# In-projection begun on one half of the tokens, an accumulator kept half by half, and V weights loaded in four pieces

## What is computed

```
# layer 0: attention, 16 heads of 32
xn = layer_norm(x) * norm_w + norm_b
att = softmax(q @ k.T + mask);  y = att @ v            # q, k, v = xn @ weights + bias
h = layer_norm(y) * (1 + scale) + shift                # scale, shift from the condition
x1 = x + silu(h) @ out_w + out_b
# layer 1: a selective state-space layer (Mamba), inner width 1024, 16 states
xn = layer_norm(x1) * (1 + scale) + shift
x_in, z = split(xn @ in_proj_w.T)
u = silu(causal_conv4(x_in) + conv_b)
dt, B, C = split(u @ x_proj_w.T);  dt = softplus(dt @ dt_proj_w.T + bias)
h_t = h_{t-1} * exp(dt_t * A) + dt_t * u_t * B_t;  y_t = sum_n(h_t * C_t)
out = x1 + gate * ((y + u * D) * silu(z)) @ out_proj_w.T
```

## Time and profile before

| | us |
|---|---|
| median of 3 runs | 6713.71 (6713.31 to 6713.74) |
| the profiled execution, its own time | 6710.81 |
| its span | 6709.0 |
| PE busy | 6107.8 (91%) |
| DVE busy | 5862.3 (87%) |
| ACT busy | 4556.3 (68%) |
| POOL busy | 3156.5 (47%) |
| mean granted TensorE clock | 0.947 |
| mean DMA rate | 162 GB/s |

### The profile page before, as it was taken

The page is one execution under the profiler, slowest core; times in us unless marked ns, Lnnn a source line. Parts: engine busy times, 40 slices in busy tenths (PEclk is TensorE's granted clock), DMA queues, the critical chain, the costliest instruction groups (busy, mean ns, idle before and its releaser), DMA issues.

```text
span 6709.0 us, 114578 instructions
## 1 busy us (share of the span) xinstructions
PE 6107.8 (91%) x43104; PEld 3983.7 (59%) x43104; DVE 5862.3 (87%) x7115; ACT 4556.3 (68%) x6528; POOL 3156.5 (47%) x1538
## 2 busy tenths in 40 slices
PE   5998999988999889989899899998899988999876
PEld 2774558645585556845568455774558645685554
DVE  0788999799997999979999799988999799996995
ACT  2775678657785677846778467865778667785663
POOL 0104881068701786019840389205881068601883
PEclk8999999999999999999999999999999999999967
DMA  3525885368934689238873498535894368924775
GB/s 143 181 82 160 203 207 153 107 163 195 236 104 141 160 205 235 77 141 177 211 200 95 135 208 209 162 98 159 196 214 142 119 162 199 244 69 144 171 149 127
DMA packets 428533, 1087.52 MB, mean 162 GB/s; under 512 B 49560, under 2 KB 49688, under 8 KB 423792
## 3 DMA queue, kind: packets, MB, share of 16 engines
q1 hardware_dynamic: 249440, 656.81, 30.2%
q0 software_dynamic: 160144, 390.09, 29.8%
q10 hardware_dynamic: 18432, 33.56, 1.4%
HBM read 570.16 MB, written 241.71 MB: 121 GB/s over the span
## 4 chain that ended last, share of the span: by engine, by line
PE 66%; DVE 16%; issue 7%; DMA 5%; POOL 4%; ACT 2%; SPq 1%; DVEq 0%; POOLq 0%; ACTq 0%
PE ps L1240 38%; PE ps L1349 12%; DVE area_h L1161 9%; PE ps L1488 8%; PE ps L1290 3%; POOL area_s L690 3%; DVE area_acc L1171 3%; DMA area_acc<-area_w 2%; DMA z_keep<-z_st 1%; DMA k_stack<-qk_keep 1%; PE ps L1292 1%; DVE area_dt L1149 1%; DVE norm_st L998 1%; DVE area_h L1129 1%; PE ps L1435 1%
## 5 line engine op out<-in xcount | busy, mean ns | idle before, releaser
L690 POOL TENSOR_TENSOR area_s<-area_u,area_s 128x1024 f32<-128x1024 f32 x1024 | 2548.6, 2578 | 536.1 <-DVE area_u L1152 372.4
L1161 DVE TENSOR_TENSOR_SCAN area_h<-ps,area_s 128x1024 f32<-128x1024 f32 x1024 | 2341.1, 2286 | 48.0 <-POOL area_s L690 39.7
L1488 PEld LDWEIGHTS ps<-ident,area_h 128*128 128x128 f32 x8192 | 987.0, 150 | 796.5 <-DVE area_acc L1171 425.5
L1488 PE MATMUL ps<-ident,area_h 128*128 128x128 f32 x8192 | 1190.5, 292 | 231.1 <-DVE area_acc L1171 152.6
L812 ACT ACTIVATE area_s<-area_s,negmax 128x1024 f32<-128x1024 f32 x1024 | 1180.7, 1153 | 253.4 <-DVE negmax L1058 245.9
L1058 DVE CUSTOM_DVE_ANT_0 area_s<-ps,area_dt 128x1024 f32<-128x1024 f32 x1024 | 1243.6, 1216 | 102.7 <-PE ps L1240 102.0
L879 ACT ACTIVATE ps<-area_dt,negA 128x1024 f32<-128x1024 f32 x1024 | 1147.0, 1120 | 240.2 <-DVE area_h L1161 102.3
L678 POOL TENSOR_TENSOR area_s<-area_s 128x1024 f32<-128x1024 f32 x64 | 180.2, 2815 | 2306.9 <-ACT area_s L854 2306.9
L863 ACT ACTIVATE area_w<-ps,C_nat 128x512 f32<-128x512 f32 x1024 | 704.9, 688 | 703.2 <-PE ps L1488 668.2
L1349 PE MATMUL ps<-ident,area_s 128*128 128x128 f32 x8192 | 1066.9, 273 | 0.4
L1349 PEld LDWEIGHTS ps<-ident,area_s 128*128 128x128 f32 x8192 | 959.9, 141 | 140.6 <-issue 7.0
(11 more groups left out here) (124 smaller groups left out, 5413.4 us busy)
## 6 DMA issues: line engine op xcount, KB each, us to landing
area_acc<-area_w POOLq DMA_DIRECT2D x256, 1024.0 KB, 8.8
area_s<-b_rows SPq DMA_DIRECT2D x256, 512.0 KB, 5.3
q_stack<-qk_keep SPq DMA_DIRECT2D x512, 128.0 KB, 2.8
k_stack<-qk_keep SPq DMA_DIRECT2D x512, 128.0 KB, 3.1
area_s<-z_keep SPq DMA_DIRECT2D x72, 512.0 KB, 4.4
qk_keep<-q_stack SPq DMA_DIRECT2D x128, 256.0 KB, 4.8
qk_keep<-k_stack SPq DMA_DIRECT2D x128, 256.0 KB, 4.8
y_keep<-area_acc POOLq DMA_DIRECT2D x8, 4096.0 KB, 13.9
```

What stands on the lines that cost most here:

```text
L690: pool.tensor_tensor(dbu[:, dl % 2, :], U[:, k // (NS * DL) * DL + dl, :], bb[:, q, :], ALU.mult).then_inc(s_dbu.sem, 1)
L1161: v.tensor_tensor_scan(out=hs[:, q, dl, :], data0=banks(2 * (dl % 2)), data1=dbu[:, dl % 2, :], initial=0.0, op0=ALU.mult, op1=ALU.add).th ...
L1488: last = nc.tensor.transpose(ps[:, 4 + n % 2, dl * P:(dl + 1) * P], hs[:, r % 2, dl, n * P:(n + 1) * P], ident[:, :])
```

## The change

Seven edits, in the code's terms:

1. **In-projection in halves.** `norm_pe` and `affine` take a half as argument. PE transposes n2's half 0 after out-projection product 6, before product 7. ACT does `affine` of half 0 after its two `root` of the next sequence's n0 and before `root(n2, b, 1)`. PE then does the token half 0 of channel groups 0 to 3, with the transposes of half 1 after group 2, and then waits for half 1. Half 1's transposes go to banks 1, 3, 5 and 7. Groups 4 to 7 run as before.
2. **n1's half 0 on ACT.** Its four normalising instructions move from DVE (L1019) to ACT, as activations; DVE keeps the shift and goes to half 1's statistics at once.
3. **Accumulator layout.** `area_acc` is now seen as (dg half, parity, 4 tiles, 512 columns). The four odd tiles of one dg are one run of 2048 words.
4. `du_keep` is stored and loaded in whole runs.
5. `y_keep` is read in two runs of 512 words for each tile instead of one of 1024.
6. **V weights** in four DMAs of 256 KB, after stores 7, 8, 9 and 10.
7. **Out-projection weights** are loaded in the attention stage, after the loads for head 13, instead of in the scan.

The diff, cut to its core:

```diff
-        acc = area_acc[:, :].rearrange("p (n d) -> p n d", n=NT)
-        piece = [acc[:, n, 512:1024] for n in range(NT)]
+        acc_parts = area_acc[:, :].rearrange("p (h e m c) -> p h e m c", h=DG, e=2, c=512)
+        acc = [acc_parts[:, :, n % 2, n // 2, :] for n in range(NT)]
+        piece = [acc[n][:, 1, :] for n in range(NT)]
...
-        n2 = Norm("norm2", n1.rows)
+        n2 = Norm("norm2", n1.rows, ((0, 1, 2, 3), (1, 3, 5, 7)))
...
-            def load_wv(inst):
-                sp.wait_ge(*s_fp.at(inst, N0_UNITS + QK_UNITS // 2))
-                sp.dma_start(wv, v_w.rearrange("(k p) c -> p k c", p=P)).then_inc(s_wv.sem, 16)
-            def load_wo(inst):
-                sp.wait_ge(*s_fp.at(inst, FIRST_V))
+            def load_wv(inst, k):
+                if k == 0:
+                    sp.wait_ge(*s_fp.at(inst, N0_UNITS + QK_UNITS // 2))
+                sp.dma_start(wv[:, k, :], v_w[k * P:(k + 1) * P, :]).then_inc(s_wv.sem, 16)
+            def load_wo():
                 sp.dma_start(wo, out_w.rearrange("(k p) c -> p k c", p=P)).then_inc(s_wo.sem, 16)
...
                         load_stack(g * HG + j + 2, j % 2)
+                load_wo()
...
-                    sp.dma_start(y_ring[:, n % 2, :], y_keep[:, n * DI:(n + 1) * DI]).then_inc(s_gyz[n % 2].sem, 16)
+                    sp.dma_start(y_ring[:, n % 2, :].rearrange("p (h c) -> p h c", h=DG), y_parts[:, :, n % 2, n // 2, :]).then_inc(s_gyz[n % 2].sem, 16)
...
-                        sp.dma_start(du_keep.rearrange("p (n d) -> p n d", n=NT), acc[:, :, 512:1024]
+                        sp.dma_start(du_keep, area_acc[:, NT * 512:]
                                      ).then_inc(s_dus.sem, 16)
...
-                        if u == QK_UNITS // 2 - 1:
-                            load_wv(b + 1)
+                        if QK_UNITS // 2 - 1 <= u < QK_UNITS // 2 - 1 + KD:
+                            load_wv(b + 1, u - QK_UNITS // 2 + 1)
                         if u == QK_UNITS - 1:
-                            load_wo(b + 1)
                             parts_stored(b + 1)
...
-                    pool.dma_start(acc_odd[:, :, dg * 512:(dg + 1) * 512], part[slot], accum_op=ALU.add
+                    pool.dma_start(acc_parts[:, dg, 1, :, :].rearrange("p m c -> p (m c)"), part[slot].rearrange("p m c -> p (m c)"), accum_op=ALU.add
                                    ).then_inc(s_ad.sem, 16)
...
+                root(n1, b, 0)
+                act.wait_ge(*n1.shift.at(b, 1))
+                _, _, _, rstd, nmr = n1.rows
+                for n in range(HALF):
+                    nc.scalar.activation(xhat[:, n, :], Y[:, n, :], ACT.Identity, bias=nmr[:, n:n + 1],
+                                         scale=rstd[:, n:n + 1]).then_inc(n1.xhat.sem, 1)
+                root(n1, b, 1)
...
                 root(n2, b, 0)
                 for hf in range(2) if b + 1 < B else ():
                     root(n0, b + 1, hf)
+                affine_n2(0)
                 root(n2, b, 1)
+                affine_n2(1)
...
-                normalise(n1, b, Y, 0)
+                shift_of(n1, b, 0)
...
                     last.then_inc(s_op.sem, 1)
-                norm_pe(n2, b)
+                    if n == NT - 2:
+                        norm_pe(n2, b, 0)
+                def in_product(n, th):
+                    for k in range(KD):
+                        done = mm(ps[:, 2 * (n % 4) + th, :], wx[:, k, n * P:(n + 1) * P],
+                                  xT[:, k, th * 512:(th + 1) * 512], k, KD - 1)
+                    return done
+                pe.wait_ge(*n2.ready.at(b, KD))
+                pe.wait_ge(*s_wx.at(b, 16))
+                for n in range(4):
+                    if n == 2:
+                        pe.wait_ge(*s_x1.at(b, NT - 1))
+                    in_product(n, 0)
+                    if n == 2:
+                        norm_pe(n2, b, 1)
                 pe.wait_ge(*n2.ready.at(b, 2 * KD))
-                pe.wait_ge(*s_wx.at(b, 16))
                 for n in range(ND):
                     if n >= 4:
                         pe.wait_ge(*s_c0.at(b, n - 3))
-                    for th in range(TB):
-                        for k in range(KD):
-                            last = mm(ps[:, 2 * (n % 4) + th, :], wx[:, k, n * P:(n + 1) * P],
-                                      xT[:, k, th * 512:(th + 1) * 512], k, KD - 1)
-                    last.then_inc(s_ip.sem, 1)
+                        in_product(n, 0)
+                    in_product(n, 1).then_inc(s_ip.sem, 1)
```

More of the change, by code:

```diff
@@ L561, in _ @@
                         sp.wait_ge(*s_gp.at(b, NU - 1))
-                        sp.dma_start(acc[:, 0:NT:2, 512:1024], du_keep.rearrange("p (n d) -> p n d", n=NT)[:, 0:NT:2, :]
+                        sp.dma_start(acc_parts[:, 1, 0, :, :], du_parts[:, 0, :, :]
                                      ).then_inc(s_dul[0].sem, 16)
@@ L567, in _ @@
                         sp.wait_ge(*s_gp.at(b, NU))
-                        sp.dma_start(acc[:, 1:5:2, 512:1024], du_keep.rearrange("p (n d) -> p n d", n=NT)[:, 1:5:2, :]
+                        sp.dma_start(acc_parts[:, 1, 1, 0:2, :], du_parts[:, 1, 0:2, :]
                                      ).then_inc(s_dul[1].sem, 16)
@@ L571, in _ @@
                         sp.wait_ge(*s_ga.at(b, 16 * NT // 2))
-                        sp.dma_start(acc[:, 5:NT:2, 512:1024], du_keep.rearrange("p (n d) -> p n d", n=NT)[:, 5:NT:2, :]
+                        sp.dma_start(acc_parts[:, 1, 1, 2:4, :], du_parts[:, 1, 2:4, :]
                                      ).then_inc(s_dul[1].sem, 16)
@@ L750, in root, with affine @@
                 nc.scalar.activation(rstd[:, rows], rv[:, rows], ACT.Sqrt).then_inc(N.rstd.sem, 1)
-            def affine(N, b, gains, shifts, func):
-                for hf in range(2):
-                    for k in range(KD):
-                        act.wait_ge(*N.tp.at(b, hf * KD + k + 1))
-                        nc.scalar.activation(xT[:, k, hf * 512:(hf + 1) * 512], ps[:, hf * KD + k, :], func,
-                                             scale=gains(k), bias=shifts(k)).then_inc(N.ready.sem, 1)
+            def affine(N, b, hf, gains, shifts, func):
+                for k in range(KD):
+                    act.wait_ge(*N.tp.at(b, hf * KD + k + 1))
+                    nc.scalar.activation(xT[:, k, hf * 512:(hf + 1) * 512], ps[:, N.banks[hf][k], :], func,
+                                         scale=gains(k), bias=shifts(k)).then_inc(N.ready.sem, 1)
             def normalise_next(inst, n):
@@ L1034, in _ @@
             for hf in range(2):
-                shift_next(0, hf)
+                shift_of(n0, 0, hf)
             for b in range(B):
@@ L1168, in add @@
                     dve.wait_ge(*s_acc.at(b, k + 1 - DL))
-                    part = acc[:, n, dg * 512:(dg + 1) * 512]
+                    part = acc[n][:, dg, :]
                     c_col = C_nat[:, n, r:r + 1] if isinstance(r, int) else C_nat[:, n, bass.ds(r, 1)]
@@ L1374, in _ @@
                 pe.wait_ge(*s_yn.at(b, G * HG * 2))
-                norm_pe(n1, b)
+                for hf in range(2):
+                    norm_pe(n1, b, hf)
                 pe.wait_ge(*s_wo.at(b, 16))
```

66 lines of the change are left out of this document (32 added, 34 removed).

## The result

The changed kernel takes **6661.6 us** (median of 4 runs, 6657.9 to 6663.5), the kernel before 6713.5 in the same session: ratio 0.9923, 95% interval [0.9906, 0.994]. The prediction said 6658.7. The number is close, but the terms that led to it are not, and most of what follows is about that.

A forecast was written before the change was run, and what follows sets the result against it. PE was taken to bound the middle of a sequence, DVE the scan. Gains of 25 + 11 + 14 + 4 + 1 = 55 us off 6710.8, plus 2.9 to the median, gave 6658.7; range 6634 to 6688.

The forecast's parts named there:

- PE's side of the halves: In-projection: PE idles 0.6 us in place of 3.9, half 1's transposes follow three half groups of 3.45 us each.
- T+24.1: Start of convolution 0, counted in us from T, the end of the out-projection; 5.7 us later than before.
- DVE's pace: Convolution: DVE becomes the bound at 5.94 us for a group with its gap; the halves gain 25 us.
- the case with the bound of 33: Upper bound of the halves' gain: without the shared port PE bounds the stage again, about 1 us more for each sequence.
- The port rule: Convolution: DVE and POOL share one port pair under exclusive lock, so a group costs both engines' work, about 6.0 us.
- It fits, barely: Ring of y and z: z lands 12.3 us after convolution 0 starts, ACT wants it after 12.9; nothing to 10 us lost.
- the ring of y and z held the convolution at a pace of 6.5: In-projection rival: the halves gain nothing and only n1's 11 us are left, 6702 us; chance 0.06.
- V pieces and layout, 14 us: Scan: three quarters of the stalls about round 9 go, 14 us; bounds 0 to 18.4.
- du_keep, 4 us: Scan, round 2: longer runs shorten the last piece that gates POOL, half a us for each sequence; bounds 0 to 12.8.
- All stalls go: Scan rival: 8 KB runs speed accumulation; round 9 stalls vanish, half of round 2's, 5 us at the tail; 6639, chance 0.11.
- n1, 11 us: Norm 1: PE starts half 1's transposes sooner and without idle time, 1.4 us in each of eight sequences; bounds 6 and 15.
- The tail: End of the kernel, where the last accumulation of 9.70 us is alone on the path: 1 us gained, bounds -1 and 6.

The follow-up runs named there:

- the kernel with the ring split: The changed kernel with z's load issued before the wait for the store and z on semaphores of its own, y still in two runs: 6622.9 us, ratio 0.987.

## Why the prediction came out right, and where it was wrong

**PE's side of the halves**: right in each step. I said convolution 0 would start at T+24.1; it starts 22.0 us after the last residual add, which is itself some 1.8 us later. I said a gap of 0.6; it is 0.61.

**DVE's pace** of 5.94 us: "it stays when PE is no longer late" held, at 5.82 us wherever POOL's gating falls beside the group. The 0.12 us too much, in 64 groups, are 7.7 us, and the kernel with the ring split gains 32.0 in these two stages where I had 25. The halves alone gain 35.4: there some groups have no gating beside them, DVE is no longer the bound and PE is, as the case with the bound of 33 supposed. The port rule's "about 6.0 us" is a wrong sum: three times 1.28 and 2.39 are 6.2, and the group takes less.

**"It fits, barely" ... "Nothing, down to 10 us lost if y lands a us later"**: this is the step that failed, and it was worth more than any term of the sum. y landed only 0.7 us later than before, and the stage lost some 47 us (569.5 with the halves alone, 616.6 in the change), not 10. I had compared one load with one deadline; it is a closed ring. By the durations of before the trip is 0.4 for issues, 4.4 for z, 1.1 for SiLU, 2.6 for gating and 2.6 for the store, 11.1 us. Before, two groups of PE took 13.8; with the halves two groups of DVE take 11.6. So the slack fell from 2.7 us to 0.5, and the halves alone already used it up (trips of 12.5 on average), which they survive only because PE allows the last groups to be late. The change then adds 0.2 for y's issue, 0.9 to z behind y, and 1.9 to the store behind late loads: 14.1 us, near the mean of 14.5 in the trace. Of the 47 us, 35 are PE waiting for U ahead of the x-projection's parts. The other 12 fall, but for half a us, in the six sequences whose mean granted clock in this stage is under 1 (0.972 to 0.988; 1.00 in all with the halves alone). The prediction had named the signs itself, convolution groups of over 6.2 us, gaps of 0.5 us or more and ACT waiting for z, and all three are there. The rival "the ring of y and z held the convolution at a pace of 6.5" named the mechanism with a chance of 0.06 and the sum of 6702 that it gives with n1 alone; I had set the ring's price as a bound of 10 us in one place and as the loss of 25 in another, and had not asked what it costs when it is late in earnest.

**V pieces and layout, 14 us**, as three quarters of the stalls: all seven are gone (18.4), and each part alone would have taken 15 us of them or more. Costing them as one term hid that one of them was nearly superfluous there. **du_keep, 4 us**: the round-2 stall gave 1.1, which is within its scatter (12.8 us before, 12.9 with the layout alone, 14.5 with the V pieces alone). **Nothing for dg 0 and the attention**: that was the other failed step. The layout alone gives 10 us in each; "runs of 8 KB make the accumulation clearly faster" stood only in the rival "All stalls go", where I let it act on stalls and the tail alone.

**n1, 11 us**: 17.4, since the clock gain was undersized. I gave it "a little sooner", but PE's 32 transposes without a gap took 5.35 us against 3.14 + 3.68 before. Between traces this stage scatters from 119.2 to 126.3 us without the edit and from 103.6 to 106.4 with it. **The tail**, 1 us: 2.4 with the start. (The "6636" among the bounds leaves out the 2.9 us to the median; it should be 6639, which changes nothing in the range.)

So, gained against predicted, +6 (n1), -37 (halves and ring), +30 (scan and attention) and -1 (the rest) cancelled to -2 us. That the forecast came so close was luck, and is no evidence for its steps.

**A better version.** Any of the three cures (y in one run, z on its own semaphores, z's load before the wait) gives 6617 to 6623 us, about 40 us under the change and some 95 under the kernel before; they can't be told apart. z's load before the wait is the smallest edit.

## What to carry to other kernels

Where tiles go around a ring (load, compute, store, load again), compare the whole trip with as many steps as there are buffers, and do it again at the pace that the change will bring: a part that speeds up the consumer and a part that slows a load by half a us can each be harmless and together cost more than either gains. Two parts that remove the same stall count once. And when a forecast comes out right, sum it by stages before believing it.

## What the runs showed that I had not expected

- In longer runs an accumulating DMA of the same 1 MB was cheaper both to issue and to land. POOL's issue of it took 1.34 us on average and takes 0.89 with the layout alone, landing went from 8.8 to 7.7, and the queue's packets (page) from 160144 before to, in the change:

```profile
q0 software_dynamic: 61840, 390.09, 26.1%
```

- The gain reaches into the attention, which issues no accumulating DMA of its own: 10 us in seven attentions, 5.9 of them in their first four tiles of 128, under which the scan's last accumulating DMAs are still running (behind the fourth sequence's scan POOL issues the last one 2.1 us after the first exponential before, and 0.2 us ahead of it with the layout alone). DVE's waits for PE's transposes (L1077) went from 73.7 to 63.5 us. What was relieved in the later tiles was not tried.
- When an earlier stage got shorter, TensorE's granted clock fell in a later one that did not change: 1.00 to 0.69 with n1 alone. What decides between the two was not tried; only that with the later gaps gone the loss is gone.
- A store issued while a load of the same queue has 3.6 us to go takes 4.9 us instead of 2.6 (medians). That is read from the traces of ring kernels, not measured by itself.
